# A four-layer graph network on one core: more destination tiles summed from gathered edge rows

## The reference

```
hypergraph:  twice  m = mean over edges of (h @ W)[src] at dst;  h = mean of m[dst] at src, + b, prelu
GRU:         red = sum over edges of h[src] + rel[type] at dst;  GRU cell(red, h)
GCN:         sum over edges, self loops too, of norm * (h @ W.T)[src] at dst, + b, layernorm, relu
attention:   softmax over the 4 heads of each edge's logits, for the first 3125 edges; weighted sum of x' [dst]
```

## Time and profile before

| | us |
|---|---|
| runs | 1287.16, 1292.99 (median), 1293.87 |
| the profiled execution | 1292.79 |
| its span | 1289.8 |
| busy: PE, PEld, DVE, ACT, POOL | 1192.9, 934.7, 701.2, 444.1, 269.8 |

### The profile page before, as it was taken

The page is one execution under the profiler, slowest core; times in us unless marked ns, Lnnn a source line. Parts: engine busy times, 40 slices in busy tenths (PEclk is TensorE's granted clock), DMA queues, the critical chain, the costliest instruction groups (busy, mean ns, idle before and its releaser), DMA issues.

```text
span 1289.8 us, 23482 instructions
## 1 busy us (share of the span) xinstructions
PE 1192.9 (92%) x9431; PEld 934.7 (72%) x9431; DVE 701.2 (54%) x1974; ACT 444.1 (34%) x948; POOL 269.8 (21%) x438
## 2 busy tenths in 40 slices
PE   2699999999999998989999999999999998999990
PEld 1456666768989995556888888676777767898970
DVE  7866456774555655545354552434435364655556
ACT  2745554428766651112112121221212222212123
POOL 6820000112000004566011110000100011355310
PEclk9989999999999999989999999999999999999995
DMA  4210000004122212322444331011101101122103
GB/s 169 73 32 1 1 2 1 1 1 162 64 69 77 76 64 81 104 77 83 127 145 167 133 113 59 25 38 32 43 25 38 37 30 55 34 59 61 36 9 101
DMA packets 48801, 80.77 MB, mean 63 GB/s; under 512 B 8617, under 2 KB 30597, under 8 KB 48688
## 3 DMA queue, kind: packets, MB, share of 16 engines
q1 hardware_dynamic: 37420, 54.52, 12.7%
q0 software_dynamic: 7136, 14.07, 3.9%
q10 hardware_dynamic: 4132, 10.63, 2.3%
HBM read 49.29 MB, written 29.89 MB: 61 GB/s over the span
## 4 chain that ended last, share of the span: by engine, by line
PE 80%; DVE 7%; POOL 6%; DMA 2%; issue 2%; ACT 2%; SPq 0%; DVEq 0%; ACTq 0%
PE ps L478 39%; PE ps L1992 11%; PE ps L817 5%; PE ps L2016 4%; PE ps L783 3%; PE ps L890 3%; PE ps L892 3%; PE ps L772 3%; PE ps L916 2%; POOL pairA L1699 2%; PE ps L896 2%; PE ps L894 2%; PE ps L862 1%; POOL whh L745 1%; POOL work L745 1%
## 5 line engine op out<-in xcount | busy, mean ns | idle before, releaser
L478 PE MATMUL ps<-big,pairB 125*128 125x250 fp8e4 (+1 forms) x2600 | 304.5, 268 | 0.6 <-DVE big L1255 0.6
L478 PEld LDWEIGHTS ps<-big,pairB 125*128 125x128 f16 x2600 | 239.6, 98 | 30.8 <-issue 2.8
L1992 PE MATMUL ps<-pairA,adj 125*125 125x512 f16 x625 | 208.1, 406 | 0.0
L727 POOL TENSOR_TENSOR st<-st,mhalf 125x1 f32<-125x1 f32 x100 | 62.0, 620 | 509.8 <-DVE st L1375 509.4
L478 PE MATMUL ps<-adj,pairB 125*128 125x250 fp8e4 (+1 forms) x1300 | 146.3, 267 | 1.8 <-DVE pairB L1433 1.8
L478 PE MATMUL ps<-adj,pairA 125*128 125x250 fp8e4 (+1 forms) x1300 | 139.2, 267 | 0.0
L478 PEld LDWEIGHTS ps<-adj,pairB 125*128 125x128 f16 x1300 | 123.3, 99 | 16.2 <-DVE pairB L1433 2.1
L478 PEld LDWEIGHTS ps<-adj,pairA 125*128 125x128 f16 x1300 | 120.9, 98 | 19.3 <-issue 7.7
L1929 ACT ACTIVATE adj<-ps 125x450 fp8e4<-125x450 f32 (+6 forms) x191 | 97.3, 518 | 103.5 <-PE ps L2018 103.0
L2018 PEld LDWEIGHTS ps<-wih 128*128 128x128 bf16 x615 | 84.6, 144 | 51.9 <-issue 1.3
L2018 PE MATMUL ps<-wih 128*128 128x7 bf16 (+5 forms) x615 | 101.9, 178 | 0.0
(11 more groups left out here) (316 smaller groups left out, 1841.8 us busy)
## 6 DMA issues: line engine op xcount, KB each, us to landing
t_adjTp<-big SPq DMA_DIRECT2D x25, 400.0 KB, 2.6
big<-t_adjTp ACTq DMA_DIRECT2D x25, 400.0 KB
t_xh<-work SPq DMA_DIRECT2D x13, 256.0 KB, 2.0
pairB<-in_x SPq DMA_DIRECT2D x5, 640.0 KB, 9.4
t_h0p<-pairB SPq DMA_DIRECT2D x5, 640.0 KB, 2.9
work<-t_xh SPq DMA_DIRECT2D x25, 128.0 KB, 2.2
xin<-t_xh SPq DMA_DIRECT2D x25, 128.0 KB, 2.2
xin<-t_x2p SPq DMA_DIRECT2D x25, 128.0 KB, 2.0
```

Source lines behind the costliest of these rows:

```text
L478: last = pe.matmul(out, src[:, j, FEAT * part + 128 * c:FEAT * part + 128 * (c + 1)], rhs(j, p), start=(n + part == 0 and not begun), stop ...
L727: g.tensor_tensor(st[:, 9:10], st[:, 8:9], k.mhalf[:, 0:1], ALU.pow).then_inc(S[rstd], 1)
L1992: last = pe.matmul(k.ps[0:P, 6 + t % 2, :], k.adj[:, j, PITCH * i:PITCH * i + P], k.pairA[:, j, :], start=(j == 0), stop=(j == TILES - 1))
```

## The change

- Lists exist for tiles 14 to 24 (`FAR` = 14), with 9 to 12 gathers each by a formula (`LISTS`), 113 in all. The mean uses those of tiles 18 to 24, the GRU all, the GCN those of 20 to 24.
- In the GRU and the GCN a listed edge block is the stationary operand and its one-hot the moving one: 4 matmuls of 125 columns (`far_sums`), so that features come out on partitions as before. The GCN adds four matmuls a tile for the self loop.
- All 113 one-hots and a scaled identity are made once, in mean2, in columns of `adj` for destination tiles 20 to 24, which nothing reads behind back1 any more.
- Slots for gathered rows: 24 in the mean, 29 and fewer in the GRU, 22 and fewer in the GCN, in buffers and in `pairA` and `pairB` rows that are not yet written. A gather waits (`F["used"]`) for the last user of its slot and for the list three before it; TensorE waits for all gathers of a list (`landed`).
- The rows gathered are first stored: `pairA` again to `pairs` in back2, `pairB` to `pairs2` in the GRU, two stores a tile on SP's queue.
- The orders of tiles change: in the mean six dense tiles come first, then a listed one after every two; in the GRU listed groups alternate with dense ones, in the GCN two are set among the dense ones and tile 24 ends.
- On GpSimd the gathers stand between the deviations by `GRU_PACE`, `GCN_PACE` and, for z0, `BASE_PACE`.
- `overlay` moves into back1's loop, `ballot` to its end, `one_hots` of the attention from GCN tile 3 to 2.

```diff
-SPARSE, EACH = 7, 10
-DENSE = TILES - SPARSE
-GATHERS = SPARSE * EACH
-AHEAD = 4
+FAR, MEAN_FAR, GCN_FAR = 14, 18, 20
+def list_length(tile):
+    share = math.sqrt((tile + 1) / TILES) - math.sqrt(tile / TILES)
+    mean = EDGES * share
+    return math.ceil((mean + 3.4 * math.sqrt(mean * (1 - share))) / SLOT)
+LISTS = [list_length(t) for t in range(FAR, TILES)]
...
-MEAN_GAPS = (4, 3, 2, 2, 3, 2, 2)
+MEAN_GAPS = (6, 2, 2, 2, 2, 2, 2)
+GRU_GROUPS = (0, 1, 2, 7, 3, 8, 4, 9, 5, 10, 6, 11, 12)
+GCN_GROUPS = (0, 1, 2, 3, 10, 4, 5, 11, 6, 7, 8, 9, 12)
+HOT_ORDER = [*range(MEAN_FAR, TILES), *range(FAR, MEAN_FAR)]
...
+GRU_PACE = (22,) + (5,) * (TILES - 1)
+GCN_PACE = (14, 3, 3, 0, 0, 3, 3, 2, 2, 3, 3, 3, 0, 0, 0, 0, 0, 2, 3, 3, 1, 0, 0, 0, 0)
+BASE_PACE = (0, 0, 0, 3, 3, 0, 0, 1, 1, 0, 0, 0, 3, 3, 3, 3, 3, 2, 0, 0, 0, 0, 0, 0, 0)
...
+    def landed(q):
+        return far_in[q % len(far_in)], 16 * sum(v.stop - v.start for v in VISITS[q % len(far_in):q + 1:len(far_in)])
...
+        def store_pair(ready, at, tile, pair, table):
+            sp.wait_ge(ready, at)
+            for a, b in ((0, 112), (112, P)):
+                sp.dma_start(table[P * tile + a:P * tile + b, :], pair[a:b, tile, :]).then_inc(M["stored"], 16)
...
+        def gather(q, n, s):
+            wait_past(pool, F["used"], max(HOME[n][1] + 1, VISITS[q - 3].stop if q >= 3 else 0))
+            g.indirect_dma_start(gathered(n), None, d["pairs2" if VISITS[q].stage == 2 else "pairs"], bass.IndirectOffsetOnAxis(ap=k.far_src[:, s:s + 1], axis=0)
+                                 ).then_inc(landed(q)[0], 16)
...
+        pool.wait_ge(M["stored"], 2 * 32 * TILES)
+        pool.wait_ge(indexed, 64)
+        waiting = gathers(1)
         for i in range(TILES):
-            deviation(i, k.st[i % 2], G, "var", "rstd", "nmr", k.dinvu)
+            for one in itertools.islice(waiting, GRU_PACE[i]):
+                gather(*one)
+            deviation(i, k.st[i % 2], G, "var", "rstd", "nmr", k.dinvu[:, GRU_ORDER[i]:GRU_ORDER[i] + 1])
+
+        pool.wait_ge(M["stored"], 3 * 32 * TILES)
+        waiting = gathers(2)
         for i in range(TILES):
+            for one in itertools.islice(waiting, GCN_PACE[i]):
+                gather(*one)
             deviation(i, k.st[i % 2], C, "var", "rstd")
             deviation(i, k.st2[i % 2], C, "var2", "rstd2", "nmr2")
-            if i == 5:
+            if i == 3:
                 pool.wait_ge(T["hot"], 1)
                 pool.wait_ge(T["base"], 16)
...
+            for t in range(sum(BASE_PACE[:i]), sum(BASE_PACE[:i + 1])):
+                g.indirect_dma_start(far_z(t), None, d["z0"][:, :], bass.IndirectOffsetOnAxis(ap=idx[:, 1, t:t + 1], axis=0)
+                                     ).then_inc(T["far"], 16)
...
+        def far_sums(stage, p, groups, bank, half, a, b):
+            tile = 2 * groups[p] + half
+            q = VISIT[stage, tile]
+            if a == 0:
+                pe.wait_ge(*landed(q))
+                pe.wait_ge(*hot_known(tile))
+            for m in range(a, min(b, LISTS[tile - FAR])):
+                x, s = gathered(VISITS[q].start + m), list_of(tile)[m]
+                for c in range(KC):
+                    at = 2 * P * c if tile == TILES - 1 else 2 * P * c + P * half
+                    for part in range(2):
+                        last = pe.matmul(k.ps[0:128, bank, at:at + P], x[:, FEAT * part + 128 * c:FEAT * part + 128 * (c + 1)], hots[s],
+                                         start=False, stop=True, skip_group_check=True)
                 last.then_inc(F["used"], 1)
...
         for p in range(NP):
+            far, pair = GRU_GROUPS[p] >= FAR // 2, len(group_tiles(GRU_GROUPS[p])) == 2
+            if far and pair:
+                far_gru(p, 1)
+            elif far:
+                far_gru(p, 0, 4)
+            else:
+                if p >= 3:
+                    gru(p, 0, 0, EARLY)
+                gru(p, 0, EARLY, TILES)
             if p >= 1:
                 turn_hold(p)
-            gru(p, 1, 0, TILES)
+            if p + 1 < NP and GRU_GROUPS[p + 1] >= FAR // 2:
+                far_gru(p + 1, 0, 0, 128 if p + 2 < NP else 4)
+            if not far:
+                gru(p, 1, 0, TILES)
             if p >= 1:
                 cell(2 * p - 2)
                 cell(2 * p - 1)
...
+            far = GCN_GROUPS[p] >= GCN_FAR // 2
+            ahead = p + 1 < NP and GCN_GROUPS[p + 1] >= GCN_FAR // 2
             for u in range(2 * TILES):
+                if far:
+                    if u % 5 == 0 and p + 1 < NP:
+                        far_gcn(p, 1, u // 5, u // 5 + 1 if u < 45 else 128)
+                elif p >= 3 or u >= EARLY:
                     gcn(p, u // TILES, u % TILES, u % TILES + 1)
+                if ahead and u % 2 == 1:
+                    n = (u - TILES) // 2 if p + 2 < NP else (u - 9) // 2
+                    if 0 <= n < LISTS[2 * GCN_GROUPS[p + 1] - FAR]:
+                        far_gcn(p + 1, 0, n, n + 1)
```

More of the change, by code:

```diff
@@ L11 @@
+import itertools
 import math
@@ L621, in load_xh @@
                 sp.wait_ge(A["x"], TILES)
-                sp.wait_ge(M["voted"], 1)
+                sp.wait_ge(F["used"], VISITS[VISIT[0, TILES - 1]].stop)
             elif p == 1:
@@ L702, in sync @@
         load_x2(0)
+        for i in (TILES - 2, TILES - 1):
+            store_pair(G["lo"], i + 1, GRU_ORDER[i], k.pairB, d["pairs2"])
         load_x2(1)
@@ L740, in gpsimd, with gathers @@
         g.tensor_tensor(k.dinv[:, 0:TILES], k.dinv[:, 0:TILES], k.mhalf[:, 0:TILES], ALU.pow).then_inc(D["root"], 1)
-        pool.wait_ge(M["stored"], 32 * TILES)
[L742 to L746, removed]
+        def gathers(stage):
+            for q, visit in enumerate(VISITS):
+                if visit.stage == stage:
+                    for n, s in zip(range(visit.start, visit.stop), list_of(visit.tile)):
+                        yield q, n, s
@@ L907, in gcn, with far_gcn @@
                     pe.wait_ge(C["copied"], p - 2)
-            last = feature_major(k, pe, bank, k.pairB, by_dst, p, c, j0, j1)
+            last = feature_major(k, pe, 1 + p % 3, k.pairB, by_dst, GCN_GROUPS[p], c, j0, j1, order=GRU_ORDER)
             if c == KC - 1 and j1 == TILES:
                 last.then_inc(C["acc"], 1)
+        def far_gcn(p, half, a, b):
+            tile = 2 * GCN_GROUPS[p] + half
+            if a == 0:
+                if half == 0:
+                    pe.wait_ge(C["copied"], p - 2)
+                    pe.wait_ge(F["hot"], GATHERS + 1)
+                for c in range(KC):
+                    for part in range(2):
+                        pe.matmul(k.ps[0:128, 1 + p % 3, 2 * P * c + P * half:2 * P * c + P * (half + 1)],
+                                  k.pairB[:, tile, FEAT * part + 128 * c:FEAT * part + 128 * (c + 1)], own_row,
+                                  start=(half + c + part == 0), stop=True, skip_group_check=True)
+            far_sums(2, p, GCN_GROUPS, 1 + p % 3, half, a, b)
         def dense_c(i):
@@ L959, in ballots @@
             pe.wait_ge(M["voted"], 1)
-            pe.matmul(k.ps[0:1, 3, 128:130 + SPARSE], k.ones[0:P, 0:1], k.votes[:, :], start=True, stop=True).then_inc(T["found"], 1)
+            pe.matmul(k.ps[0:1, 3, 128:130 + len(LISTS)], k.ones[0:P, 0:1], k.votes[:, :], start=True, stop=True).then_inc(T["found"], 1)
         def keep_warm(n):
@@ L1055, in degree, with copy_out @@
                          accum_out=(k.odeg8, k.rsD4)[n][:, i:i + 1]).then_inc(A["degree"], 1)
-        def copy_out(S, bank, p, scale=1.0, early=None):
-            act.wait_ge(S["acc"], p + 1)
+        def copy_out(S, bank, p, scale=1.0, early=None, far=None):
+            if far is not None and far[1][p] >= far[2] // 2:
+                act.wait_ge(F["used"], VISITS[VISIT[far[0], group_tiles(far[1][p])[-1]]].stop)
+            else:
+                act.wait_ge(S["acc"], p + 1 if far is None else sum(g < far[2] // 2 for g in far[1][:p + 1]))
             if p >= 2:
@@ L1070, in scale_high @@
             i = MEAN_ORDER[t]
-            if i >= DENSE:
-                act.wait_ge(F["used"], EACH * (i - DENSE + 1))
+            if i >= MEAN_FAR:
+                act.wait_ge(F["used"], VISITS[VISIT[0, i]].stop)
             else:
@@ L1456, in vector @@
             flip_out(f)
+        dve.wait_ge(built["padded"], 1)
+        own.link(v.memset(k.over, 0))
         dve.wait_ge(D["root"], 1)
@@ L1471, in vector @@
                     after_g(2 * p - 1)
+                if n in (2, 6):
+                    overlay(2 * p + n // 4)
             if p == 8:
@@ L1498, in vector @@
                 source_keys()
-        ballot()
         skip_bias(0)
```

242 lines of the change are left out of this document (153 added, 89 removed).

## The result

The changed kernel took 1331.99 us (4 runs, 1330.08 to 1333.66), the kernel before 1291.41 (4 runs): 1.031 times as long, interval 1.028 to 1.034. 1284 us and no more than 1303 had been predicted. The same kernel was then run again on four chips, each time beside the kernel before (which chip the recorded result came from is not known).

| occasion | the changed kernel | before | ratio (interval) |
|---|---|---|---|
| first, the recorded one | 1331.99 (4 runs) | 1291.41 | 1.031 (1.028 to 1.034) |
| e5 | 1291.19 (9) | 1290.95 | 0.9996 (0.998 to 1.001) |
| e9 | 1291.83 (8) | 1292.46 | 0.9996 (0.998 to 1.001) |
| e16 | 1291.43 (8) | 1291.36 | 0.9997 (0.998 to 1.001) |
| e11 | 1346.17 (2) | 1289.75 | 1.044 (1.037 to 1.051) |

The account below looks back on a forecast made before the run. TensorE was taken to bound the first scatter, GRU and GCN, with GpSimd binding the GCN after the change. Second mean -17.7, GRU -21.4 and GCN +31 gave -8.1 us, from 1292.8 to 1284.7, stated as 1284; range 1262 to 1303.

Parts of the forecast that it names:

- -17.7: Second mean: TensorE's waits for gathered rows and the slow matmuls behind them go, -17.7 us; -9 if half the lists come late.
- -21.4: GRU: listed tiles save TensorE 33.7 us, less a 10.5 us wait for tile 24's list and 1.8 of VectorE lag.
- -33.7: GRU: TensorE's work saved by listed instead of dense tiles, 59.5 us going and 25.8 coming; also the term's lower bound.
- Rival (c): GRU and GCN: gathers cost 1.5 us beside VectorE, making 1299 us; chance 0.11.
- +31: GCN: GpSimd's in-order queue of gathers and deviations becomes the bound, 201.7 us for 170.6, so +31 us.
- 9 behind turn 20: GCN's end: 9 us added to GpSimd's queue because TensorE sets the pace again for the last four tiles.
- +25 and +36: GCN: bounds of its term, for 1.25 us a gather and 3.41 a deviation, or 1.37 and 3.62.
- the signs of being wrong: GCN of 170 us or less, gaps between its gathers for TensorE, its clock under 0.95, or gather waits in several GRU groups.
- TensorE loses 15.4 us: GCN tiles 20 to 24: listed work takes TensorE 12.1 us for 27.2, but no gain expected since GpSimd becomes the bound.
- rival (a): GCN: GpSimd does not bind, only the late start costs and TensorE's saving is had, 1249 us; chance 0.14.
- rival (b): GCN: TensorE's granted clock falls through its waits, costing up to 20 us, 1304 us; chance 0.13.
- "same": Whole kernel: a change of less than 0.5%, 6.5 us, hardly told from none; chance 0.27.

Follow-up runs that it names:

- e5: The changed kernel itself run again, nothing changed, beside the kernel before; 1291.19 us (9 runs), ratio 0.9996.
- e9: The changed kernel itself run again for a third occasion, nothing changed; 1291.83 us (8 runs), ratio 0.9996.
- e16: The changed kernel itself run again, beside the kernel before, to know which kind of occasion it was; 1291.43 us (8 runs), ratio 0.9997.
- e11: The changed kernel itself run again for a fourth occasion, nothing changed; 1346.17 us (2 runs), ratio 1.044.
- e14: e8 with waits for landings after every sixth of the second mean's first 24 gathers, short products after every sixth of the GRU's first 22; 1301.3 us, one execution.
- e4: The changed kernel with tile 24's first four slots in the GRU put behind the cells of tiles 20 and 21 in TensorE's order; 1280.8 us.
- e2: The changed kernel with three short GpSimd products after every sixth of the first 24 gathers of the second mean and first 22 of the GRU; 1291.3 us.
- e8: e4 with the GCN's gathers spread evenly over the tiles, one of them between a tile's two powers; 1259.4 us, 0.974 times the kernel before.
- e3: The changed kernel without the GCN's 48 edge gathers, old rows summed in their place; 1265.4 us.
- e10: e3 with the z0 gathers two to a tile from tile 5 on, instead of three in some tiles; 1259.3 us.

## Why the prediction was wrong, by its steps

**What failed: "-17.7" and "-21.4", by something that was no rival.** Both terms take TensorE's saving whole but for waits on lists, and set at nothing what a long run of gathers does to TensorE where no list is late. Between the recorded trace and that of e5 lie 40.5 us: 18.1 before the GRU, 24.1 in it, -1.7 behind it. In the second mean and the GRU TensorE stands 27.9 us with no wait ("issue") in the recorded trace and never in e5, and its busy time is 11.2 us longer, at a granted clock of 0.93 and 0.95 for 1.00 and 0.98. This is slow issue. The rivals all spoke of GpSimd's queue, the clock and the price of a gather. e14 ties it to the unbroken run; that it depends on the chip or the occasion is shown; why is open. The kernel before takes the same on the occasions with slow issue (1289.75 in e11, 1298.1 in e14, one execution). Its longest run of gathers is 20 in 27.4 us, with a wait of TensorE of 4.47 us in it, and the others are of 12 and fewer; whether gaps come in that run there, no trace shows.

**The same two terms where there is no slow issue: right.** In e5 the second mean takes 112.7 us (483.5 to 596.2) with no wait for `t_pairs`, "about 113" as predicted; of the 21.2 us up to the GRU 2.0 had come before the mean, as these stages vary by that much between traces. The 17.8 us taken off also held a third stop, 4.01 us at 513.84, which the prediction does not name. GRU -21.5 for -21.4, with one wait of 10.66 us where 10.5 was worked out; e4 gives it back. TensorE's busy time in the stage fell by 35.7 us in e4, at full clock (302.7 to 267.0), for "-33.7". The overlay costs nothing: the mean began 483.5 to 485.9 us into the span in e2 to e8, at 485.5 before.

**Rival (c).** It falls: the median gather keeps 0.95 + 0.30 us in the GRU and the GCN. Beside its own 1.30 the prediction worked out 1.37 there by the rule of the Trainium skill (SBUF — State Buffer, "SBUF: two separate sides"). The shut-out is there, but small. In e5 ten gathers of the GRU take 1.14 us, each where an instruction of VectorE with two inputs in SBUF begins 0.36 us into it:

```profile
820.78 1.14 POOL L849 DMA_INDIRECT big<-t_pairs,far_src  x1 [0.30 <-issue]
821.14 0.43 DVE L1607 TENSOR_TENSOR work<-big,xin 125x256 f32<-125x256 f32 x1
```

17 others that begin 0.35 to 0.37 us after such an instruction (L1614, 0.42 us) take 0.94 or 0.95. In the GCN only 9 of the 48 edge gathers have one beside them in their first 0.7 us, and none takes more than 1.03 us. So what counted was when the two meet and how long VectorE's instruction is (0.98 us for an overlay), not how busy VectorE is, 94 of 208 us.

**GCN: +31 became +37.7.** GpSimd was the bound, as said (e3). Up to turn 20 the queue took 180.2 us (1258.2 - 1078.0) for 178.7 worked out. The mis-sized term is the end, "9 behind turn 20" on top of four deviations of 3.5: 23 us, but 28.4 were needed. The kernel before needs 24.6 us for them already (1224.56 to 1249.13), and tile 24's listed group has little work of TensorE beside a tile's chain; that this is the reason was not tried. The rest behind the last deviation grew by 3.0 in e5, where 0 was taken. By the prediction's own figures its bounds are +26.4 and +37.5, not +25 and +36; the measured one lies above both. Some of its signs came otherwise in e5: the granted clock of the stage was 0.89, which stood among the signs of being wrong, TensorE's busy share was 82% for 75%, and `turn_h` waited for ScalarE in 12 tiles, not in almost every one.

**"TensorE loses 15.4 us".** (27.2 - 12.1 are 15.1.) It would not have been had without the queue either, as rival (a) took it: without any edge gather the stage takes 180.8 (e3) or 175.3 us (e10), longer than the 170.6 before. A dense group gives the chain of a tile 13.6 us of other work to lie beside, a listed one about half, by the estimate ahead of e10; TensorE then waits for ScalarE's tile inside it, and the clock, 0.94 over the stage, takes more. The clock's part is rival (b)'s mechanism, smaller than there. That it is what holds e8 at 187.2 us fits TensorE's busy time there, but was not tried alone.

**The range.** Without slow issue the kernel lies at 1288.9 to 1293.5 us, inside 1262 to 1303 and in the "same" that had 0.27. With it, it lies outside; a range that left this out could not hold it. The gain of 8 us did not come on any occasion: without slow issue the GCN and the rest behind it took 9.7 us more than the sum had.

## What to carry to other kernels

Count what each queue must do per tile before moving work to it, and put it where that queue waits anyway: a gather between the two powers was free, and moving 19 of them there, some 25 us of GpSimd's queue, with a shorter start, made the stage 18.7 us shorter. Work taken off the bounding engine is lost where it was the cover of another chain. Break long runs of gathers by waits for their landings, as few as the lists allow; that this helps rests on one trace (e14). Time such a kernel on more than one chip before believing either sign.

## What the runs showed of the hardware that was not expected

- On three of twelve occasions (the recorded one, e11, e14) TensorE's instructions went out in steps of 0.70 us during long runs of gathers, from 16 to 21 us (mean) or 9 us (the GRU's start) after the start of the run until 3 to 4 us behind its last gather. On the others a run of up to 66 left no gap. Two chips were met twice, both times without. Up to the first gap TensorE has 151 to 177 recorded instructions in both stages, though its rates differ by two; but in the runs of 20 gathers with deviations between, they are 273 to 318, and a run of 26 in the GCN of e14 left no gap. So no count is claimed.
- It was not a late block of instructions: the trace's queue for them fetched 16 KB at 489.5 us and next at 531.9, with 249 recorded instructions between, and mostly 225 to 290 lie between two fetches elsewhere, so it was asked for after the usual count of instructions. The Trainium skill (Runtime: NRT & Kernel Launch, "Instruction fetch mechanics") says that crossing from one block of 16 KB to the next is mostly hidden. The trace agrees: in e5 a fetch at 516.8 us falls into 18 us in which TensorE is busy for 18.00. Slow issue has another cause, which stays open.
- The median gather costs 0.95 us and 0.30 ahead of it in every stage (e5). One of VectorE's 0.42 us instructions with two inputs in SBUF adds 0.2 us if it begins 0.36 us into the gather.
